# A mixture's weighted sum, its input and its norm: from a stage of their own to the experts' store and the next attention

## The reference

```python
x = x + attention0(norm(x), ctx)                      # a0
x = x + mixture0(norm(x))                             # m0
x = x + attention1(norm(x), ctx)                      # a1
x = x + quantum_ffn(norm(x))                          # f1
x = x + window_attention(ctx, norm(x))                # w2
x = x + mixture2(norm(x))                             # m2
x = x + attention3(norm(x), ctx)                      # a3
x = x + ternary_ffn(norm(x))                          # f3

def mixture0(xf):            # 8 experts, 2 per token
    gates = softmax(xf @ gate_w); topw, topi = top_k(gates, 2)
    topw = topw / sum(topw)                           # of each token
    y_e  = gelu(ln(xf @ w1[e] + b1[e]) * g1 + bt1) @ w2[e] + b2[e]
    return ln(topw[0] * y_topi0 + topw[1] * y_topi1 + xf) * ln_g + ln_b
def mixture2(x):             # 8 experts, 2 per token
    v, i = top_k(x @ router_w.T, 2); w = softmax(v)
    y_e  = gelu(x @ w1[e].T + b1[e]) @ w2[e].T + b2[e]
    return w[0] * y_i0 + w[1] * y_i1
```

## Time and profile before

| | us |
|---|---|
| median of three executions | 2499.39 |
| lowest, highest | 2496.64, 2502.64 |
| the profiled execution, device time | 2496.09 |
| its span (first to last record) | 2494.3 |
| mean granted TensorE clock of it | 0.879 of 2.4 GHz |
| busy: TensorE, VectorE, ScalarE, GpSimd | 1960.8, 1378.0, 894.4, 522.7 |

### The profile page before, as it was taken

How to read it: one execution, slowest core, us unless ns; L and a number is a source line. 1 busy time by engine, 2 the same in 40 slices (tenths; PEclk the granted TensorE clock), 3 DMA queues, 4 the chain that set the end, 5 groups by cost and what they waited for, 6 DMA issues and landing times. The chain is left out here.

```text
span 2494.3 us, 40430 instructions
## 1 busy us (share of the span) xinstructions
PE 1960.8 (79%) x11858; PEld 1467.3 (59%) x11859; DVE 1378.0 (55%) x3378; ACT 894.4 (36%) x1938; POOL 522.7 (21%) x560
## 2 busy tenths in 40 slices
PE   6997419999800699699979751999999994999587
PEld 4665406666500366366666441899999993565255
DVE  5875426666467477778756443222222222787787
ACT  3452104444311344333312110333333332545587
POOL 1212532211187111101100164000000004562000
PEclk9997559999955799899989655999999996999699
DMA  6000231221121400000000323111111113110001
GB/s 243 1 1 22 80 132 57 63 62 61 56 74 58 180 1 1 13 1 0 0 8 10 135 89 108 30 38 34 38 35 36 38 34 121 39 47 1 8 27 35
DMA packets 81874, 125.70 MB, mean 50 GB/s; under 512 B 17104, under 2 KB 65872, under 8 KB 78704
## 3 DMA queue, kind: packets, MB, share of 16 engines
q1 hardware_dynamic: 46640, 68.02, 8.2%
q0 software_dynamic: 13104, 35.80, 4.4%
q10 hardware_dynamic: 22032, 20.62, 2.4%
HBM read 82.58 MB, written 41.81 MB: 50 GB/s over the span
## 5 line engine op out<-in xcount | busy, mean ns | idle before, releaser
L1386 ACT ACTIVATE e_hT<-psum,e_bt 128x128 f32<-128x128 f32 x568 | 154.2, 383 | 335.3 <-PE psum L1349 335.3
L1349 PEld LDWEIGHTS psum<-e_xT,e_w 128*128 128x128 f32 x2272 | 267.0, 193 | 8.4 <-ACT e_xT L1379 4.9
L1349 PE MATMUL psum<-e_xT,e_w 128*128 128x128 f32 x2272 | 267.7, 276 | 4.2 <-ACT e_xT L1379 4.2
L1358 PE MATMUL psum<-m_w,e_hT 128*128 x1136 | 256.8, 379 | 0.0
L268 POOL TENSOR_TENSOR rstd<-lnt,half 128x4 f32<-128x4 f32 (+1 forms) x72 | 75.6, 1050 | 760.9 <-DVE lnt L262 760.8
L1358 PEld LDWEIGHTS psum<-m_w,e_hT 128*128 128x128 f32 x1136 | 210.4, 190 | 25.7
L1414 DVE COPY e_w<-m_w 128x2048 f32 x71 | 87.1, 1227 | 250.0 <-PE psum L1349 224.6
L698 DVE TENSOR_REDUCE a_mx<-psum 128x8 f32<-128x512 f32 x192 | 123.2, 684 | 109.4 <-PE psum L502 109.1
L483 PE MATMUL psum<-a_cx,att_wk 128*128 128x64 f32 x192 | 29.9, 305 | 165.0 <-DMA a_cx<-in_ctxT 165.0
L1212 ACT ACTIVATE e_hT<-psum,e_bt,e_gt 128x128 f32<-128x128 f32 x284 | 106.7, 456 | 140.8 <-PE psum L1175 140.8
L627 ACT ACTIVATE a_pT<-psum 128x512 f32<-128x512 f32 x192 | 104.0, 594 | 127.3 <-PE psum L552 127.2
(11 more groups left out here) (275 smaller groups left out, 3898.4 us busy)
## 6 DMA issues: line engine op xcount, KB each, us to landing
e_x<-sorted_in SPq DMA_DIRECT2D x142, 128.0 KB, 2.2
sorted_out<-e_y ACTq DMA_DIRECT2D x142, 128.0 KB, 1.7
m_w<-in_L_ffn_w SPq DMA_DIRECT2D x16, 1024.0 KB
m_w<-in_L_ffn_w SPq DMA_DIRECT2D x16, 512.0 KB
x_res<-in_x SPq DMA_DIRECT2D x8, 512.0 KB, 7.1
out_x<-x_res SPq DMA_DIRECT2D x8, 512.0 KB, 2.9
a_cx<-in_ctxT SPq DMA_DIRECT2D x40, 64.0 KB, 2.3
e_b<-in_L_ffn_b SPq DMA_DIRECT2D x2, 1024.0 KB, 4.2
```

What stands on the lines that cost most here:

```text
L1349: mm = pe.matmul(h_b[s][:, f, :], w1[:, kk, f * P:(f + 1) * P], xT[s][:, kk, :], start=(kk == 0), stop=(kk == DC - 1))
L1358: mm = pe.matmul(y_b[s][:, 0:D], hT[s][:, f, :], k.w2[:, bass.ds(e * (FC * D) + f * D, D)], start=(f == 0), stop=(f == FC - 1))
L1386: g = act.activation(hT[s][:, f, :], h_b[s][:, f, :], ACT.Gelu, bias=bt[:, bass.ds(e * FC + f, 1)])
```

## The change

**Rows that carry their weight.** A row of `sorted_in` has 259 floats (`ROW`): the 256 features and three that VectorE writes in the dispatch's `route`: the smaller weight (`W_LEAST`), the difference of the two (`W_MORE`), and the code of the first chosen expert (`W_CODE`). For that the gap, its Exp on ScalarE and the weights are made per batch inside the loop, and not once at the end; the first mixture too copies the tokens into two `zk` buffers and keeps no `z`. GpSimd's scatter waits for the weights too. In the experts VectorE makes the weight of each row from these three and the tile's owner (`row_weight`, two small instructions a tile) and, in the first mixture, adds the input row to the result; ScalarE multiplies the tile by the weights before it stores it. So `sorted_out` holds w * (y + x_normalised), and, since a token's two weights make 1, the sum of its two rows is the mixture's sum with its input. The loops' bodies hold six tiles (first mixture) or four (second), and loads run six tiles ahead in the first.

**Accumulating gathers.** `Arrival` gathers the second choice on top of the first (`compute_op=add`), waiting for the first to land. In a3 both are added onto x itself. In a1 the first is copied into one of two buffers `u` of four tiles, the second added; then statistics and moments on VectorE, root on GpSimd, `normalise_sum` on ScalarE, the gain `post_g` on GpSimd (`scale_sum`), the addition to x on VectorE (`add_sum`), and the statistics of x. `combine`, `combine_norm` and the two sums of the old `Arrival` are gone. In a1 the statistics of x stay after tile 3 of a batch, those of the sum come after tile 0; in a3 the statistics move to after tile 1.

```diff
@@ class Arrival
+    def gather(self, pool, j, b, adding):
+        for n in range(b * TPB, (b + 1) * TPB):
             pool.indirect_dma_start(
+                out=self.at(n), out_offset=None, in_=self.k.ys[:, :],
+                in_offset=bass.IndirectOffsetOnAxis(ap=self.k.pos[j][:, n:n + 1], axis=0),
+                compute_op=ALU.add if adding else ALU.bypass).then_inc(self.k.y_in[j][b], 16)
+    def fetch_first(self, pool, b):
+        if self.normed:
+            wait_pos(pool, self.x_done, b - 1)
+        self.gather(pool, 0, b, not self.normed)
+    def fetch_second(self, pool, b):
+        self.landed(pool, 0, b)
+        self.gather(pool, 1, b, True)
+    def sum_statistics(self, dve, b):
+        self.landed(dve, 1, b)
         for n in range(b * TPB, (b + 1) * TPB):
+            self.u_norm.statistics(dve, n, self.at(n))
+        self.u_norm.moments(dve, b)
+    def normalise_sum(self, act, b):
+        act.wait_ge(self.u_norm.centred, b + 1)
+        for n in range(b * TPB, (b + 1) * TPB):
+            o = act.activation(self.at(n), self.at(n), ACT.Identity, bias=self.u_shift[:, n:n + 1],
+                               scale=self.k.rstd[:, n:n + 1])
+        o.then_inc(self.u_done, 1)
+    def scale_sum(self, pool, b):
+        u = self.u[b % 2]
+        pool.wait_ge(self.k.post_in, 16)
+        pool.wait_ge(self.u_done, b + 1)
+        pool.tensor_tensor(u[:, :, :], u[:, :, :], self.k.post_g[:, None, :].to_broadcast([P, TPB, D]),
+                           ALU.mult).then_inc(self.u_scaled, 1)
+    def add_sum(self, dve, b):
+        dve.wait_ge(self.u_scaled, b + 1)
+        dve.tensor_tensor(xs, xs, self.u[b % 2][:, :, :], ALU.add).then_inc(self.x_done, 1)
@@ attention, GpSimd
+                if normed:
+                    arrival.fetch_first(pool, 0)
+                    arrival.fetch_second(pool, 0)
+                    arrival.fetch_first(pool, 1)
+                    arrival.u_norm.root(pool, 0)
+                    arrival.scale_sum(pool, 0)
+                    arrival.fetch_second(pool, 1)
+                    in_norm.root(pool, 0)
+                    arrival.u_norm.root(pool, 1)
+                    arrival.scale_sum(pool, 1)
+                    in_norm.root(pool, 1)
+                    fetch(2)
+                elif arrival:
+                    fetch(0)
+                    arrival.fetch_first(pool, 1)
+                    arrival.fetch_first(pool, 2)
+                    arrival.fetch_second(pool, 1)
+                    in_norm.root(pool, 0)
+                    arrival.fetch_first(pool, 3)
+                    arrival.fetch_second(pool, 2)
+                    in_norm.root(pool, 1)
...
                 for b in range(NB):
+                    if normed and b + 2 < NB:
+                        arrival.u_norm.root(pool, b + 2)
+                        if b + 3 < NB:
+                            arrival.fetch_first(pool, b + 3)
+                        arrival.scale_sum(pool, b + 2)
+                        if b + 3 < NB:
+                            arrival.fetch_second(pool, b + 3)
+                    if arrival and not normed:
+                        if b + 4 < NB:
+                            arrival.fetch_first(pool, b + 4)
+                        if b + 3 < NB:
+                            arrival.fetch_second(pool, b + 3)
@@ attention, ScalarE
-                        if arrival and b + 2 < NB and t < 2:
-                            for i in range(2):
-                                arrival.scale_first(act, (b + 2) * TPB + 2 * t + i)
+                        if normed and b + 2 < NB and t == 1:
+                            arrival.normalise_sum(act, b + 2)
@@ attention, VectorE
+                        if normed and b + 2 < NB and t == 0:
+                            arrival.sum_statistics(dve, b + 2)
+                        if normed and b + 2 < NB and t == 2:
+                            arrival.add_sum(dve, b + 2)
+                        if arrival and not normed and b + 2 < NB and t == 1:
+                            arrival.statistics(dve, b + 2)
@@ dispatch, ScalarE
+                    act.wait_ge(gap_done, b + 1)
+                    act.activation(odds[:, tiles], gap[:, tiles], ACT.Exp).then_inc(gap_exp, 1)
                 over_batches(act, step)
-                act.wait_ge(gap_done, 1)
-                act.activation(k.wt[1][:, :], gap[:, :], ACT.Exp).then_inc(gap_exp, 1)
@@ dispatch, VectorE, route, before the counting, and after the row numbers
+                    dve.tensor_tensor(gap[:, tiles], top[1][:, tiles], top[0][:, tiles], ALU.subtract).then_inc(gap_done, 1)
...
+                    dve.wait_ge(gap_exp, b + 1)
+                    n = then(n, dve.tensor_scalar(den[:, :], odds[:, tiles], 1.0, None, ALU.add))
+                    dve.wait_ge(z_kept, b + 1)
+                    n = then(n, dve.reciprocal(den[:, :], den[:, :]))
+                    n = then(n, dve.tensor_tensor(zk[s][:, :, W_LEAST], odds[:, tiles], den[:, :], ALU.mult))
+                    dve.tensor_tensor(zk[s][:, :, W_MORE], den[:, :], zk[s][:, :, W_LEAST], ALU.subtract).then_inc(w_kept, 1)
+                    dve.tensor_copy(zk[s][:, :, W_CODE], code[0][:, :]).then_inc(w_kept, 1)
@@ experts_norm, VectorE, a tile
+                    row_weight(dve, k, xin[r], wv[:, r:r + 1], j, w_part).then_inc(w_known, 1)
                     dve.wait_ge(y_ps, j + 1)
+                    dve.tensor_tensor(y[s][:, :], y_b[:, 0:D], b2[:, bass.ds(e * D, D)], ALU.add).then_inc(y_read, 1)
+                    dve.wait_ge(y_read, j + 1)
+                    dve.tensor_tensor(y[s][:, :], y[s][:, :], xin[r][:, 0:D], ALU.add).then_inc(y_done, 1)
@@ both experts, ScalarE, store
+                    act.wait_ge(w_known, j + 1)
+                    act.activation(y[s][:, :], y[s][:, :], ACT.Copy, scale=wv[:, r:r + 1]).then_inc(y_scaled, 1)
+                    act.wait_ge(y_scaled, j + 1)
```

505 lines of the change are left out of this document (195 added, 310 removed).

## The result

The changed kernel takes 2505.15 us (median of 14, 2502.56 to 2506.54) against 2499.13 (14 runs) for the one before: ratio 1.0022, interval 1.0014 to 1.0029. It is slower by 6 us, or 0.2%, where 2459 was forecast. The profiled execution has a span of 2503.6 us where 2494.3 was.

A forecast was written before the change was run, and what follows sets the result against it. Bound by stage lengths, TensorE idle in the 144 us between experts and second attention. Removing `combine_norm` gave -142.5, added costs left -40.6: span 2494.3 and execution 2496.1 to 2455.5, median 2459, range 2425 to 2500.

The forecast's parts named there:

- First experts: First mixture's experts: VectorE's added 0.9 us a tile hides in 1.37 of waits; only ScalarE's last scaling shows, +0.6.
- rival 2: First experts: VectorE becomes the bound, 0.4 us a tile if additions run slower beside GpSimd, 28 us: 2487; chance 0.12.
- Rival 4: First experts: longer loops stall at each jump back, ten jumps at 5.7 us cost 57: 2516; chance 0.03.
- Accumulating gather: Second and fourth attention: an accumulating gather issues and lands like a plain one, 0.96 us with 0.31 to the next.
- rival 1: Both attentions: accumulating gather costs twice the issue, 2.5 instead of 1.25 us, +89: 2548; decides from about 0.55; chance 0.10.
- Landing: Second attention's start: gathers land 7.1 us after their start beside weight loads, 2.85 with empty queues; start +45.7.
- Second attention's body: Second attention, first to last softmax: +9.9, and +3 for batch 2 fetched late; a period of 24 to 25 us.
- the order that I blamed: Second attention: statistics of x after tile 3 delay the softmax chain; that order cost the fourth attention 8.4 us.
- Its end and the fourth attention's body: Second attention's end: next stage starts late after gathers, +5.4; fourth attention's body: sums leave and statistics move, -8.
- both mechanisms: Dispatch: ScalarE's copy waits behind the Exp, 1.45 us a batch; VectorE's five small steps 1.0; +17 for each mixture.
- my 2.45 a batch: Dispatch: 1.45 us for the Exp's wait and 1.0 for VectorE's small instructions, in each of seven batches.
- its own terms: Whole kernel: forecast 2459 taken as 2438 to 2482 from dispatch 7 to 30 each, start +33 to +46, slips +12.

## Why the prediction was wrong, point by point

- **Removed stage**: -142.5, right by construction, since it is the length of a stage that is gone.
- **First experts**: the step that failed. "1.37 a tile, so 0.5 is left: hidden" took a wait put down to TensorE for free time of VectorE. Of the 1.37 all but 0.33 us was time in which the sequencer loaded the tile's expert and worked out waits, against 0.9 of work added, and 0.78 of it stayed when nothing was waited for. VectorE became the bound, as rival 2 had it, and "if additions run slower beside GpSimd" was the right mechanism for 15 us of the 31. Rival 2 gave +28 for this term with a chance of 0.12 and it came as 31.4; that the sizes are so near is in part luck, since rival 2 didn't have the sequencer's time or the jumps. Rival 4's jumps cost 0.57 each and not 5.7.
- **Accumulating gather**: "I take its issue and landing as those of the plain one" failed by 0.59 us a gather, which is past the 0.55 from which rival 1 was to decide. It is nearly all of the 19.5 us missed at the fourth attention's start (19.2 came off without it, 4.2 of it through the later landing), and 10 of the second's.
- **Landing**: 7.1 was taken from a start where 3 MB were loaded; the second attention's start had 8.8, then 12.8, then, with the loads through, 3.8; the fourth's had 10.6 once, and 3.9 for batch 1.
- **Second attention's body**: 25.6 a batch for 24 to 25, +7.5; the order that I blamed isn't the cause by itself, as two runs show; it counts for 0.75 us a batch once VectorE has less to do (25.1 to 24.35).
- **Its end and the fourth attention's body**: +5.4 and -8.4 for +5.4 and -8; right.
- **Dispatch**: both mechanisms were there, the sum too large, 34 for 20. The first placement-to-placement time grew by 2.66 us (10.56 to 13.22), as my 2.45 a batch had it, the third to the sixth by 1.3 to 1.7. The stretch of 16.3 us didn't come again: the placement that followed at 260.16 after 243.84 now follows at 261.90 after 246.99, 14.9. I had added my 2.45 us to a stretch that took them in.
- **In sum**: two rivals that I had held apart, each with a chance near 0.1, both came in part. Their conditions (0.5 us of slack a tile, 0.55 us a gather) were both thin. The range to 2500 held rival 2 alone (2487), but neither rival 1 nor the two together. The bounds named for "its own terms" also add up to 2426 to 2497 and not to 2438 to 2482.

## What to carry to other kernels

A wait in a profile is not slack: before work is laid into it, read the sequencer's own rows and subtract what it does in that time; tiles whose code is written out show the pitch without the part that comes from loop registers. An accumulating gather saves an addition and costs issue time on GpSimd and a wait for the landing of what it adds onto; in the fourth attention's steady loop that was hidden (22.45 us a batch, TensorE's pace), at the start of a stage both are paid, and the more while weights are loaded beside it, and there plain gathers into spare buffers and one addition are better. Where VectorE is near its bound, GpSimd operations on SBUF beside it cost most of their length (15.5 us for 16 of 1.26).

## What the runs showed of the hardware

- A 128 x 256 float gather on GpSimd: 0.95 us plain, 1.54 accumulating, 0.30 to the next. Landing of a group of four after its last start: 3.2 plain and 4.1 accumulating with the later weights held back; beside weight loads 6.4 to 8.8 plain, 10.6 and 12.8 accumulating.
- A VectorE step of 0.22 us beside a GpSimd addition on SBUF ended with it, after 1.21.
- The load of a tile's expert into a register takes VectorE's sequencer 0.30 us, and 0.19 and 0.02 for what follows it. Loop registers cost VectorE some 0.28 us a tile more than code written out (4.40 against 4.12), a jump back 0.57.
- At a granted clock of 0.94 and not 1.00 a batch of attention took 27.1 us and not 25.6.
